# Normalisation sums taken with a factor of minus one over the width, in a fused Mamba and MoE block on one core

## The reference, cut to what matters

```python
h = layernorm(x) * (1 + ca) + sa                 # first norm
h = layernorm(h) * norm_scale + norm_bias        # second norm, inside the attention part
# h @ W_in, convolution, silu, softplus, scan over time with 16 states, gate, @ W_out
x = x + ga * (h + that)
h = layernorm(x) * (1 + cb) + sb                 # third norm
x = x + gb * moe(h)                              # 16 experts, router with top 4

def layernorm(x):
    m = mean(x, axis=-1); v = var(x, axis=-1)
    return (x - m) / sqrt(v + 1e-5)
```

## Time and profile before

| | us |
|---|---|
| median of three runs | 2883.38 |
| lowest and highest | 2881.95, 2892.45 |
| the profiled execution | 2885.27 |
| its span, from the first to the last instruction | 2883.5 |
| VectorE busy | 2467.0 (86%) |
| TensorE busy | 2415.4 (84%) |
| GpSimd busy | 2232.1 (77%) |
| ScalarE busy | 1569.0 (54%) |

### The profile page before, as it was taken

The page is one execution under the profiler, slowest core; times in us unless marked ns, Lnnn a source line. Parts: engine busy times, 40 slices in busy tenths (PEclk is TensorE's granted clock), DMA queues, the critical chain, the costliest instruction groups (busy, mean ns, idle before and its releaser), DMA issues.

```text
span 2883.5 us, 29133 instructions
## 1 busy us (share of the span) xinstructions
PE 2415.4 (84%) x9004; PEld 1719.6 (60%) x9004; DVE 2467.0 (86%) x2514; ACT 1569.0 (54%) x2945; POOL 2232.1 (77%) x1515
## 2 busy tenths in 40 slices
PE   3444897989889798988979798897979889797889
PEld 1222575656657565665756566675656657565678
DVE  2588998989899898989989898998989899898932
ACT  3556565565556556555655655565565556655310
POOL 1578888788888888888887888888788888877922
PEclk8667898989999898999989899998989999898999
DMA  4678888887888888888898888888887878987931
GB/s 116 175 188 223 211 225 224 204 217 208 209 218 221 219 207 216 211 211 207 222 227 202 216 210 209 214 222 227 211 201 208 209 209 222 229 203 200 240 73 49
DMA packets 337373, 584.75 MB, mean 203 GB/s; under 512 B 50224, under 2 KB 153136, under 8 KB 337216
## 3 DMA queue, kind: packets, MB, share of 16 engines
q1 hardware_dynamic: 281920, 381.54, 42.5%
q0 software_dynamic: 55296, 201.35, 36.2%
HBM read 371.38 MB, written 10.06 MB: 132 GB/s over the span
## 4 chain that ended last, share of the span: by engine, by line
PE 38%; POOL 18%; DVE 16%; issue 13%; ACT 8%; DMA 6%; SPq 0%; POOLq 0%; DVEq 0%; ACTq 0%
PE wbank L476 12%; PE mbank L488 7%; DVE hbank L705 7%; POOL unit L1129 7%; PE wbank L380 4%; PE wbank L418 4%; DMA gsum<-unit 3%; DVE unit L712 3%; POOL gsum L1152 3%; PE wbank L504 3%; POOL act L1117 3%; DMA ht<-in_L_attn_x_dram 2%; PE wbank L368 2%; ACT hbank L980 1%; PE wbank L438 1%
## 5 line engine op out<-in xcount | busy, mean ns | idle before, releaser
L1129 POOL TENSOR_TENSOR unit<-dtx,b_bc 128x1024 f32<-128x1024 f32 x512 | 1306.4, 2565 | 34.3 <-DMA b_bc<-bc_scratch 29.7
L705 DVE TENSOR_TENSOR_SCAN hbank<-hbank,unit 128x1024 f32<-128x1024 f32 x512 | 1172.9, 2291 | 36.8 <-ACT hbank L980 31.4
L980 ACT ACTIVATE hbank<-dt,a_neg 128x512 f32<-128x512 f32 x1024 | 668.7, 680 | 289.1 <-DVE unit L712 286.2
L712 DVE TENSOR_TENSOR unit<-hbank,c_bc 128x1024 f32<-128x1024 f32 x512 | 624.1, 1219 | 26.5 <-DMA c_bc<-bc_scratch 0.5
L488 PE MATMUL mbank<-down_t,act 128*128 128x256 f32 x2048 | 516.8, 392 | 67.2 <-POOL act L1117 67.2
L1117 POOL TENSOR_TENSOR act<-act,w_all 128x512 f32<-128x512 f32 x256 | 356.4, 1392 | 271.9 <-DVE act L684 253.6
L476 PE MATMUL wbank<-h_t,gate_t 128*128 128x256 f32 x2048 | 504.5, 390 | 9.8 <-DVE xb L569 9.6
L488 PEld LDWEIGHTS mbank<-down_t,act 128*128 128x128 f32 x2048 | 395.3, 195 | 167.6 <-POOL act L1117 83.3
L476 PE MATMUL wbank<-h_t,up_t 128*128 128x256 f32 x2048 | 486.0, 380 | 1.1 <-DVE act L677 0.6
L1152 POOL DMA_DIRECT2D gsum<-unit x384 | 370.4, 965 | 128.3 <-DVE unit L712 72.6
L476 PEld LDWEIGHTS wbank<-h_t,gate_t 128*128 128x128 f32 x2048 | 400.4, 197 | 110.5 <-issue 33.7
(11 more groups left out here) (118 smaller groups left out, 2479.3 us busy)
## 6 DMA issues: line engine op xcount, KB each, us to landing
gsum<-unit POOLq DMA_DIRECT2D x384, 512.0 KB, 7.4
b_bc<-bc_scratch SPq DMA_DIRECT2D x512, 256.0 KB, 5.7
c_bc<-bc_scratch SPq DMA_DIRECT2D x512, 256.0 KB, 5.4
w_all<-w_scratch SPq DMA_DIRECT2D x256, 256.0 KB, 4.3
ht<-in_L_attn_x_dram SPq DMA_DIRECT2D x16, 512.0 KB, 8.1
xt<-in_L_attn_x_dram SPq DMA_DIRECT2D x16, 512.0 KB, 6.6
out_dram<-xt SPq DMA_DIRECT2D x16, 512.0 KB, 3.3
z<-mod_scratch SPq DMA_DIRECT2D x16, 256.0 KB, 8.7
```

What stands on the lines that cost most here:

```text
L705: eng.tensor_tensor_scan(h, h, unit[:, g % RING, :, :].rearrange("p a t -> p (a t)"), 0.0, ALU.mult, ALU.add).then_inc(scanned, 1)
L712: eng.tensor_tensor(unit[:, g % RING, :, :], hbank[g % HB][:, :, :], c_bc[:, s:s + 1, :].to_broadcast([P, 2, T]), ALU.mult).then_inc(c_sca ...
L980: eng.activation(hbank[g % HB][:, a, :], dt[:, 2 * q + a, :], ACT.Exp, scale=a_neg[:, 2 * q + a, n:n + 1]).then_inc(decayed, 1)
L1129: eng.tensor_tensor(unit[:, g % RING, :, :], dtx[:, 2 * q:2 * q + 2, :], b_bc[:, s:s + 1, :].to_broadcast([P, 2, T]), ALU.mult).then_inc(d ...
```

## The change

`row_sums` becomes `row_means` on ScalarE. It passes `scale = -1/H`, so that the accumulator holds the negated mean, and it writes it straight into `nmean`. Its elementwise result goes to `z2[:, q % 2]` and no longer in place. GpSimd's `row_means` and the buffers `sums` and `sums2` are gone. Each of the four activations now signals, the third and fourth wait for the first and second, and the first square waits for all four means, on ScalarE's own semaphore. The steps of the generators keep their number and places.

```diff
-            def row_sums(src, out, done):
-                for q in range(TT):
-                    i = eng.activation(src[:, q, :], src[:, q, :], ACT.Identity, accum_out=out[:, q:q + 1])
-                i.then_inc(done, 1)
-            def row_squares(src, mean, out, done, at):
+            def row_means(src, mean, done, at):
                 for q in range(TT):
                     if q >= 2:
                         need.wait_ge(done, at + q - 1)
+                    eng.activation(z2[:, q % 2, :], src[:, q, :], ACT.Identity, scale=-1.0 / H,
+                                   accum_out=mean[:, q:q + 1]).then_inc(done, 1)
+            def row_squares(src, mean, out, done, at):
+                for q in range(TT):
+                    need.wait_ge(done, at + max(q - 1, 0))
                     eng.activation(z2[:, q % 2, :], src[:, q, :], ACT.Square, bias=mean[:, q:q + 1],
                                    accum_out=out[:, q:q + 1]).then_inc(done, 1)
...
             def stats(row):                                     # ScalarE
-                row_sums(x1, sums2, rnorm_a)
-                yield
-                yield
-                need.wait_ge(rnorm_p, 4 * row + 1)
-                row_squares(x1, nmean2, squares2, rnorm_a, 5 * row + 1)
+                row_means(x1, nmean2, rnorm_a, 8 * row)
+                yield
+                yield
+                row_squares(x1, nmean2, squares2, rnorm_a, 8 * row + 4)
...
-            def row_means(total, mean, made):                   # GpSimd
-                eng.tensor_scalar(mean[:, :], total[:, :], -1.0 / H, None, ALU.mult).then_inc(made[0], 1)
...
             def stats(row):                                     # GpSimd
-                need.wait_ge(rnorm_a, 5 * row + 1)
-                row_means(sums2, nmean2, (rnorm_p, 4 * row))
-                yield
-                yield
-                need.wait_ge(rnorm_a, 5 * row + 5)
-                row_scales(squares2, ve2, nmean2, rstd2, shift2, (rnorm_p, 4 * row + 1))
+                yield
+                yield
+                need.wait_ge(rnorm_a, 8 * row + 8)
+                row_scales(squares2, ve2, nmean2, rstd2, shift2, (rnorm_p, 3 * row))
```

## The result

The changed kernel took 2904.45 us in the median (2902.56 to 2905.95), the kernel before 2883.57 us on the same chip (2881.95 to 2892.45). The ratio is 1.0056, with a 95% interval of 1.0039 to 1.0073, so the change costs 11 to 21 us. The forecast was 2879.5 us with a range up to 2889. It was wrong in size and in sign.

A forecast was written before the change was run, and what follows sets the result against it. No engine alone was taken as the bound, but a chain of waits over all engines. Gains of 1.0 + 0 + 1.9 + 1.0 = 3.9 us took the median from 2883.4 to 2879.5 us, range 2873 to 2889.

The forecast's parts named there:

- the drive ends: Sign of being right, third norm: without nmean, GpSimd's drive ends 2.4 us after the DMA issue.
- In the first norm nothing is saved: First norm of later rows: ve still waits for the squares, so GpSimd's idle time only moves before ve; gain nothing.
- The added waits: ScalarE's new waits among means and squares: taken as costing nothing, at most 8 us, since a decay covers them.
- The sum of 3.9 us: Whole gain: 1.0 third norm, 0 first norm, 1.9 second norm, 1.0 first and last row.
- the third norm's term: GpSimd's drive and ve come 0.20 us earlier in 11 steady rows; bounds 0.8 and 2.2 us, taken as 1.0.
- The prediction's own sign of being wrong: Would show it wrong: ScalarE idle before first square or third mean, more late `ht` landings, or VectorE's scans waiting.
- The slower rival: First norm's accumulating DMA, issued earlier, delays the load of `ht` by 2.4 us a row; up to 2913 us, chance 0.07.
- the DMA released in the first norm: First norm: without nmean's wait GpSimd issues its 512 KB accumulating DMA some 4.6 us earlier, meeting other transfers.
- The price for 14 rows, 34 us: The slower rival's full size: all 14 steady rows late by 2.4 us, giving 2913 us.
- The range: 2873 to 2889 us, allowing two or three more or fewer late loads of 2.4 us and the runs' upward tail.
- The second norm's 1.9 us: Second norm, 12 chain rows: 7 gain 0.20 us, 5 about 0.1 where squares hold ve; bounds nothing and 2.4.

The follow-up runs named there:

- e4: Changed kernel with one idle [128, 4] GpSimd instruction where the third norm's nmean stood; 0.9989 of the kernel before.
- e2: Only the first and second norm have the change, the third keeps nmean on GpSimd; 0.9992 of the kernel before.
- e9: Changed kernel with one idle instruction at the third norm's nmean place and two before the second accumulating DMA; 0.9981 of the kernel before.
- e10: Changed kernel with three idle instructions before the second accumulating DMA, none in the third norm; 2879.59 us, 0.9971 of the kernel before.
- e11: Kernel before with two idle instructions before the second accumulating DMA; 0.9973 of the kernel before.
- e7: Changed kernel with the load of `ht` issued one unit earlier on SyncE; 1.0019 of the kernel before.
- e8: Kernel before with the load of `ht` issued one unit earlier on SyncE; 1.0020 of the kernel before.
- e5: Changed kernel with one idle instruction right before the second accumulating DMA only; 0.9981 of the kernel before.
- e1: Only the third norm has the change, the first and second keep GpSimd's nmean; 1.0072 of the kernel before.
- e3: Changed kernel with GpSimd again waiting for the first norm's means, so the third accumulating DMA goes out late; 1.0037 of the kernel before.
- e12: The changed kernel itself, run again on the chip of e9 to e11; 1.0052 of the kernel before.
- e6: Changed kernel with two idle instructions at nmean's old place in the third norm; 1.0096 of the kernel before.
- e13: e6 with two more idle instructions before the second accumulating DMA; 1.0075 of the kernel before.

## Why the prediction was wrong

**What was right.** In the third norm the drive ends at 1629.20 + 2.66 = 1631.86, 2.39 us after the DMA issue's end at 1629.47, as forecast. In the first norm nothing is saved: ve's idle time went from 1.23 us to 7.16, where the prediction had "from 1.23 to about 6 us". The added waits cost nothing that can be seen. In the groups by line of ScalarE (count, busy, mean ns, idle before) the squares have hardly any idle time left in front of them, and the means take 404 ns as the sums did:

```profile
L808 ACT ACTIVATE z<-xt 128x256 f32<-128x256 f32 x64 | 25.8, 404 | 115.3 <-DVE xt L600 115.3
L815 ACT ACTIVATE z<-xt,nmean 128x256 f32<-128x256 f32 x64 | 31.5, 494 | 0.0
```

At the very first norm the squares follow the means with 0.03 us between them, where there were 0.44:

```profile
13.23 0.19 ACT L808 ACTIVATION_READ_ACCUMULATOR z<-ht 128x1 f32 x1
13.45 0.51 ACT L815 ACTIVATE z<-ht,nmean 128x256 f32<-128x256 f32 x1
```

The sum of 3.9 us is not contradicted: e4 and e2, which take back or leave out the third norm's part, are at 0.9989 and 0.9992, some 3 and 2 us faster than before, and their intervals reach from 6 us faster to 1 us slower. Once both kernels have the second DMA moved out (e9, e10 and e11) or the load moved up (e7 and e8), they can't be told apart.

**The step that failed** is the third norm's term, +1.0 us in the sum. It said of the load: "The issue follows VectorE's and SyncE's work and not the third norm, so it does not move with it." That is true, and it is the reason for the loss and not for calm. GpSimd's row moved by 0.2 us and SyncE's did not, so the two accumulating DMAs behind the third norm moved against the load. The term counted what the 0.20 us brings to ve and the drive, and nothing for the two DMA issues that moved with them against SyncE's queue. It is the second of the two, 2.8 us behind the load's issue, whose move costs the time (e5). The change in the third norm alone costs 0.72% (e1), which is 21 us (16 to 26), where the term had a gain of 1.0. The prediction's own sign of being wrong, "landings of `ht` above 8.1 us in more rows than now", is what came.

**The slower rival was the right one with the wrong culprit.** It named the place ("any later landing counts in full"), the price (2.4 us a row) and the shape of the evidence. But it hung on the DMA released in the first norm, which e2 and e3 clear, and its case against was "a transfer of the same kind, issued before the load, is in flight beside it today". That transfer is the first DMA, and at -0.41 us it is still nearly harmless (e5 and e10). The one that hurts is the next, issued behind the load, which the prediction doesn't speak of. The prediction also had the released DMA go out 4.6 us earlier. Beside the load it went out 2.8 us earlier (7.52 us behind the load's issue and not 10.33), since it now waits for the landing of the first DMA:

```profile
1642.68 0.87 POOL L1138 DMA_DIRECT2D gsum<-unit  x1 [1.86 <-DMA gsum<-unit]
```

The price for 14 rows, 34 us, was too high, since three rows are late before and a late row costs some 2 us. That this rival named the right kind of loss is partly luck, since another DMA was the cause.

**The range** allowed for late loads changing "by two or three" rows, since "a load's landing is decided by 0.1 us". Nine changed. The flips were priced as if each row had its own chance, but all steady rows have the same phase within 0.04 us, so a shift moves them together.

**The second norm's 1.9 us** was read from rows in which VectorE and GpSimd had the phase of before. In the changed kernel ve at the second norm follows a DMA issue, which ends at 1665.43 + 1.19 = 1666.62, and not the squares:

```profile
1665.43 1.19 POOL L1138 DMA_DIRECT2D gsum<-unit  x1
1666.70 0.19 POOL L1042 TENSOR_SCALAR ve<-squares 128x4 f32<-128x4 f32 x1
```

Its worth alone was not measured.

**What stays open.** From the issue of the last load to the end the changed kernel's profile takes 423.1 us (2904.2 - 2481.1) against 415.7 before (2883.5 - 2467.8). That is 7.4 us, more than one late load; in e12 it is 3.3 us, and I have no cause for the rest. On the same chip e1 is some 9 us slower than e3, with intervals that don't meet and only one late row more; the first and second norm's own gain may be part of it, and the rest has no cause here. Why a first DMA at 0.00 us makes the load late when at -0.2 and -0.4 it does not is shown as a fact (e6, e13) and not explained, nor why 2.82 and 3.06 us differ so sharply for the second, when its packets begin at the same time in both kernels. Nor is it known why 3 or 4 rows of the 13 are late at 3.06 us and the others not. The records don't say which of the 16 DMA engines a packet is on. So the phase as the cause of the late loads, and the late loads as the cause of the loss, are shown by experiments (e1 to e5, e7 to e11), and what happens inside the DMA engines is only read from the records.

## What to carry to other kernels

When an instruction goes from an engine's row, follow that row on to every DMA that it issues, and compare their times with the transfers of the other queues that have no slack. If the pattern repeats in every row, price the shift for all rows at once. A transfer whose user waits on it with 0.1 us of slack is the first thing to free, and the cheapest cure can be a delay of the one that collides with it, as in e10 and e11, and not an earlier issue, as in e7 and e8.

## What the runs showed of the hardware

- A 512 KB load lands 8.1, 10.5 or 11.3 us after its issue, depending on how two accumulating DMAs of 512 KB on another queue lie beside it, and a shift of 0.24 us decides between the first two in most rows (9.0 us or more in 12 of 13 rows of the changed kernel and in 4 of 13 of e4). It is not monotonic: from the changed kernel over e4 to e6, later is first better and then worse.
- A [128, 4] instruction on GpSimd delays what stands behind it by some 0.2 us (the second DMA from 2.82 to 3.07 us in e5), although its record may show 0.5 us.
- A wait of ScalarE on its own semaphore right behind the instruction that signals it left 0.03 us of idle time (13.42 to 13.45 us).
- VectorE's `r_two`, a [128, 48] operation on line 619, took 0.20 us in the median before and 1.85 us in e8, where it runs beside GpSimd's drive. The times are min, median and max in ns, of before and of e8:

```profile
L619 DVE TENSOR_TENSOR r_two<-r_ch x16: 200/201/2598, 294.1 to 2781.6; 128x48 f32<-128x48 f32 x16
```

```profile
L619 DVE TENSOR_TENSOR r_two<-r_ch x16: 198/1851/2605, 288.4 to 2791.8; 128x48 f32<-128x48 f32 x16
```

In the row of e8 shown above, VectorE's timeline has it start while the drive (1636.75 to 1639.10) is under way, and end at 1639.17, just after it:

```profile
1637.62 1.55 DVE L619 TENSOR_TENSOR r_two<-r_ch 128x48 f32<-128x48 f32 x1
```

The Trainium skill, "SBUF — State Buffer", section "SBUF: two separate sides", says that VectorE operations with two SBUF inputs and GpSimd operations that read SBUF share a port pair as an exclusive lock, the later one waiting for the whole of the other. The trace agrees, with the operation over 0.07 us after the drive. It is so in all 13 rows of e8 in which the drive is under way when `r_two` starts; in the one where `r_two` starts 0.02 us before the drive it takes 0.20 us. The lock was not tested by a run of its own.
